# Batch-owned buffers, seven shared PSUM banks, and one searched order for all engines in a four-stage attention kernel

## The chip, the cores and the metric

The kernel runs on one core of one Trainium2 chip. The metric is device time in microseconds (us), the median of several runs; lower is better. The core has TensorE (PE, with a separate record for its weight loads), VectorE (DVE), ScalarE (ACT) and GpSimd (POOL), each with its own instruction stream in program order, and SyncE (SP), which here issues most of the DMAs.

## The reference

Four batches (B = 4) of 256 tokens with 128 channels go through attention layers with 16 heads of 8 channels. Cut to what is computed:

```python
x = attn0(x, ctx) + x                        # rotary positions on q and k, softmax over 256 keys
mod = silu(ctx[:, :2]) @ ada_w + ada_b       # 9 vectors for each half: shift, scale, gate, three times
x0, x1 = halves of x (128 tokens each)
xh = xh + g_msa * mha(mod(ln(xh)))           # each half attends to itself (128 keys)
xh = xh + g_mca * mha(mod(ln(xh)), other)    # each half attends to the other half
xh = xh + g_mlp * (gelu(mod(ln(xh)) @ fc1) @ fc2)
x = ln(attn3(x, ctx) + x) * g + b            # softmax over 256 keys
x = x + attn4(ln(x) * g + b, ctx)            # weights quantised to -1, 0, 1 times their mean size
```

So there are five attentions per batch, called phases 0 to 4 below. Phases 1 and 2 are those on halves. A pair (phase, batch) is a unit; there are 20.

## The kernel before

**One unit.** q and k are projected (fp32), and each is split into three bf16 parts. Six DMAs for q and six for k place the parts in every eighth partition of `q_stack` and `k_stack`, in pairs that make up an fp32 product (`SLOTS`), two more slots being constants that were loaded at the start (`in_spare`). A bank (128 x 512 fp32 in PSUM) of products q k is made by PE from 64 partitions, the next bank from the other 64. DVE takes its row maxima (`neg_max`, L1294). There are 16 such banks in a unit of phases 0, 3 and 4 and 8 in one of phases 1 and 2, 256 in all. The maxima are split into two bf16 parts (`max_parts`, L715 and L717), transposed by PE, copied out (L727 or L1205) and placed by DMA in two rows of `q_stack`. Then PE makes the scores with keys on partitions (`ps_score`, 256 banks), ACT takes their exponentials (`probs`, L1155, 8 buffers), and PE multiplies with `v_cols` in column tiles of 32 (`ps_heads`, `value`, 160 steps of 4 products). Then come a copy (L1162), the transpose `unstack`, the division (L1363, L1364), `heads_t`, the output projection `out_proj`, the addition of `base` (L1374), the statistics of the norm (L1258 to L1263), the reciprocal deviation on POOL (L908), the norm itself (`normed`, L735, on DVE in phases 0 to 2 and on POOL in phase 3) and its transpose `norm_t`, from which the next phase of that batch starts.

**Order.** `make_schedule` builds one list of steps by a planner with fixed costs (`Plan`) that always takes the ready step that is earliest after a bonus per stream (`WEIGHTS`). Every engine runs its part of that one list in order; much of what DVE, ACT and POOL do has no place of its own but stands where the PE step that feeds it stands. Units come in a fixed order: all batches of phase 0, then of phase 1, and so on.

**Buffers.** They go by the unit's turn: two of `neg_max`, parts, `base`, three of the stacks and of `v_cols`, one of `heads_raw`, `heads`, `normed`. The PSUM banks are private to a kind of work: three for `ps_max`, two for `ps_score`, one for `ps_heads`, two for all else (`ps_small`).

**Start and gates.** The rotary table's rows are gathered by 8 indirect DMAs (16 floats per token), widened on DVE (L1302) and transposed by PE. The three gates of each of 8 batch halves are a product with a replicated silu (`silu_rep`), 8 times [128 x 384]; POOL then multiplies them into `gated_o` and `gated_fc2` (`gate_fold`, L877 to L883).

Nearly all products of PE are recorded at L937, the helper `mm`; they are told apart by their tiles.

Of the kernel before, what the change touches and what calls it, by code (L numbers as in the profile page):

```python
# [22 lines left out]
UNITS = PHASES * B  # L23
# [3 lines left out]

UNIT = tuple((phase, b) for phase in range(PHASES) for b in range(B))
PHASE = tuple(phase for phase, b in UNIT)
BATCH = tuple(b for phase, b in UNIT)  # L30
AT = {unit: u for u, unit in enumerate(UNIT)}
BEFORE = tuple(AT.get((phase - 1, b)) for phase, b in UNIT)

SLOTS = ((0, 2), (1, 1), (2, 0), (0, 1), (1, 0), (0, 0))


ROW_SLOTS = 8
SPARE_SLOTS = (6, 7)
HALF = P // 2
MAX_ROW = HALF - 2  # L40
STACK_BUFS = 3
BANK = 512
CHUNK = BANK
SMALL_BUFS, MAX_BUFS, SCORE_BUFS = 2, 3, 2
# [24 lines left out]
ROPE_COLS = 2 * DH  # L69


def halves(u):

    return PHASE[u] in (1, 2)


def n_banks(u):
    return PAIRS if halves(u) else 2 * PAIRS


def n_chunks(u):
    return PAIRS if halves(u) else H


def n_groups(u):

    return 2 if u in GROUPED else 1


def quad_of_chunk(n):  # L90

    u = 0
    while n >= n_chunks(u):
        n -= n_chunks(u)
        u += 1
    return u, n * 4 // n_chunks(u)


def on_dve(work, u):

    return (work, PHASE[u]) in ON_DVE


def splitter(kind, u):

    return "dve" if (kind, PHASE[u]) in SPLIT_ON_DVE or u < 1 else "pool"

OFF_PE = {"norm": None, "apply": None, "stats": None, "max_split": None, "stack_max": None, "expand": None,  # L110
          "split_q": "pool", "split_k": "pool", "gate_fold": "pool", "quantise": "pool",
          "stack_q": "dma", "stack_k": "dma"}

LAG = {"pe": 200, "act": 180, "dve": 130, "pool": 70, "dma": 2150}
# [4 lines left out]
            "max_t0": 270, "max_t1": 270}  # L121


ROW_BANK, ROW_ISSUE, DRAIN = 225, 12, 170


class Plan:
# [8 lines left out]
    def run(self, engine, after, cost, gelu=False):  # L136

        if engine == "act" and gelu != self.gelu:
            self.gelu, cost = gelu, cost + 1300
# [1328 lines left out]
```

## Time and profile before

| what | us |
|---|---|
| median of 3 runs | 361.76 (361.42 to 364.45) |
| the profiled execution: its span, first to last instruction | 356.7 |
| between that span and the median | 5.1 |

The page of the profile gives busy time per engine, the span in slices, and the costliest groups of instructions. Busy time of PE counts each product with its modelled latency, so a PE that is called busy may still be waiting for most of that time. The granted clock (PEclk) is 1.00 where TensorE has 2.4 GHz and 0.50 where it has 1.2 GHz; a window's figure is the mean of the two.

### The profile page before, as it was taken

How to read it: one execution, taken by the hardware profiler on the slowest of the kernel's cores; microseconds unless marked ns; L12 is line 12 of the kernel's file. 1: busy time of each engine (PE TensorE's matmuls, PEld its weight loads, DVE VectorE, ACT ScalarE, POOL GpSimd, SP SyncE). 2: the span in 40 equal slices, each digit the busy share in tenths (PEclk: the TensorE clock that was granted, in tenths of full speed). 3: DMA queues.
4: the chain of work that ended last, by engine and by line, in shares of the span. 5: the costliest groups of instructions: out<-in, count | busy, mean ns of one | idle time of the engine just before them, and what ended most of it. 6: DMA issues, size and time to landing. Idle time of an engine off the chain costs nothing.

```text
span 356.7 us, 8841 instructions
## 1 busy us (share of the span) xinstructions
PE 303.9 (85%) x3162; PEld 169.3 (47%) x3162; DVE 246.3 (69%) x551; ACT 233.3 (65%) x491; POOL 187.3 (53%) x273
## 2 busy tenths in 40 slices
PE   3187899789899689788988989899888999898993
PEld 2173444345436466556666656455343534344331
DVE  2679599989746657758738487857686879778411
ACT  1131275767878378576768586787787777676782
POOL 3876498968888555336254332403676675740000
PEclk9587699999999899899899989879999999999999
DMA  2769700303032122133132111200212112130000
GB/s 70 184 164 244 249 9 5 83 10 79 16 83 68 33 75 75 50 77 91 27 91 54 39 47 48 60 9 19 74 38 58 51 41 69 37 78 18 17 17 16
DMA packets 40563, 22.95 MB, mean 64 GB/s; under 512 B 4872, under 2 KB 39688, under 8 KB 40392
## 3 DMA queue, kind: packets, MB, share of 16 engines
q1 hardware_dynamic: 39832, 22.30, 23.9%
q8 instruction: 25, 0.41, 0.5%
q0 software_dynamic: 256, 0.07, 0.2%
q14 instruction: 18, 0.15, 0.1%
q10 hardware_dynamic: 432, 0.02, 0.1%
HBM read 5.79 MB, written 0.52 MB: 18 GB/s over the span
## 4 chain that ended last, share of the span: by engine, by line
PE 30%; DVE 6%; ACT 6%; POOL 5%; issue 5%; SPq 1%; DMA 1%; POOLq 0%; ACTq 0%; DVEq 0%
PE ps_small L937 9%; PE ps_heads L937 7%; PE ps_max L937 5%; PE ps_score L937 5%; POOL normed L735 3%; ACT probs L1155 2%; DVE neg_max L1294 2%; PE ps_small L1108 2%; POOL rstd L908 1%; PE ps_small L1112 1%; DVE stats L1258 1%; PE ps_small L1122 1%; SPq L793 1%; DVE normed L735 1%; ACT L1228 1%
## 5 line engine op out<-in xcount | busy, mean ns | idle before, releaser
L1294 DVE TENSOR_REDUCE neg_max<-ps_max 128x2 f32<-128x512 f32 (+1 forms) x256 | 159.8, 682 | 38.4 <-PE ps_max L937 37.7
L1155 ACT ACTIVATE probs<-ps_score 128x512 f32<-128x512 f32 x256 | 141.4, 600 | 29.5 <-PE ps_score L937 28.5
L937 PE MATMUL ps_score<-q_stack,k_stack 64*128 64x256 bf16 (+1 forms) x640 | 78.8, 258 | 6.6 <-ACT probs L1155 4.3
L937 PE MATMUL ps_heads<-probs,v_cols 128*32 128x256 f32 (+1 forms) x1280 | 83.1, 350 | 0.6 <-ACT probs L1155 0.4
L937 PE MATMUL ps_max<-k_stack,q_stack 62*128 62x256 bf16 (+1 forms) x640 | 72.0, 259 | 7.9 <-DVE neg_max L1294 4.1
L937 PEld LDWEIGHTS ps_score<-q_stack,k_stack 64*128 64x128 bf16 x640 | 34.1, 96 | 40.9 <-ACT probs L1155 29.0
L937 PEld LDWEIGHTS ps_max<-k_stack,q_stack 62*128 62x128 bf16 x640 | 33.3, 96 | 41.2 <-DVE neg_max L1294 22.8
L937 PEld LDWEIGHTS ps_heads<-probs,v_cols 128*32 128x32 f32 x1280 | 28.3, 109 | 25.4 <-issue 17.3
L702 POOL TENSOR_TENSOR split_r<-q_f,k_parts 128x256 f32<-128x256 f32 x19 | 12.8, 673 | 46.2 <-issue 41.9
L937 PE MATMUL ps_small<-src_t,w 128*128 128x256 f32 x96 | 30.0, 433 | 0.9 <-issue 0.5
L908 POOL TENSOR_TENSOR rstd<-var_eps,minus_half 128x2 f32<-128x2 f32 x20 | 14.2, 708 | 30.8 <-DVE var_eps L1263 30.6
L702 POOL TENSOR_TENSOR split_r<-q_f,q_parts 128x256 f32<-128x256 f32 x19 | 12.7, 670 | 24.6 <-issue 23.2
L937 PEld LDWEIGHTS ps_small<-src_t,w 128*128 128x128 f32 x96 | 17.8, 207 | 8.7 <-issue 4.6
L1181 ACT ACTIVATE q_f<-ps_small,vec 128x256 f32<-128x256 f32 x32 | 15.2, 474 | 9.6 <-PE ps_small L937 9.2
L1219 ACT ACTIVATE src_t<-ps_small,mods 128x128 f32<-128x128 f32 x24 | 9.7, 453 | 15.2 <-PE ps_small L1122 15.2
L902 POOL TENSOR_TENSOR base<-x,rows 128x256 f32<-128x256 f32 x12 | 8.7, 726 | 19.0 <-DVE x L1374 18.2
L1363 DVE RECIPROCAL inv_sum<-ps_small 128x32 f32<-128x32 f32 x20 | 7.0, 352 | 15.6 <-PE ps_small L1108 15.3
L1162 ACT ACTIVATE heads_raw<-ps_heads 128x512 f32<-128x512 f32 x20 | 12.0, 602 | 5.5 <-PE ps_heads L937 5.1
L937 PE MATMUL ps_small<-ctx_t,w 128*128 128x256 f32 x32 | 11.5, 471 | 4.8 <-DMA ctx_t<-in_ctx_t 4.2
L1122 PE MATMUL ps_small<-ident_f,normed 128*128 128x128 f32 x32 | 6.9, 298 | 9.5 <-DVE normed L735 8.0
L1108 PE MATMUL ps_small<-ident_f,heads_raw 128*128 128x128 f32 x80 | 12.6, 280 | 2.0 <-ACT heads_raw L1162 2.0
L937 PE MATMUL ps_small<-w,ctx_t 128*128 128x128 f32 x48 | 9.2, 320 | 5.8 <-issue 5.8
(112 smaller groups left out, 420.6 us busy)
## 6 DMA issues: line engine op xcount, KB each, us to landing
k_stack<-k_parts SPq DMA_DIRECT2D x120, 64.0 KB, 2.1
q_stack<-q_parts SPq DMA_DIRECT2D x120, 64.0 KB, 2.1
w<-in_w SPq DMA_DIRECT2D x1, 1024.0 KB, 5.8
rows<-in_rows SPq DMA_DIRECT2D x1, 704.0 KB, 5.0
w<-in_w SPq DMA_DIRECT2D x1, 576.0 KB, 8.6
q_stack<-max_rows SPq DMA_DIRECT2D x36, 8.0 KB
ctx_t<-in_ctx_t SPq DMA_DIRECT2D x4, 128.0 KB, 3.5
src_t<-in_x_t SPq DMA_DIRECT2D x4, 128.0 KB, 3.6
```

The lines of the kernel that those rows point to most:

```text
L702: link(ops.tensor_tensor(rest, full, part[0], ALU.subtract))
L735: last = ops.tensor_scalar(normed[:, qt, :], src[:, qt, :], mean_var[:, qt, 0:1], rstd[:, qt:qt + 1], ALU.subtract, ALU.mult)
L902: nc.gpsimd.tensor_tensor(base[:, u % 2, :, :], x[:, b, :, :], add, ALU.add).then_inc(base_ready, 1)
L908: nc.gpsimd.tensor_tensor(rstd[:, :], var_eps[:, :], minus_half[:, :], ALU.pow).then_inc(rstd_ready, 1)
L937: return nc.tensor.matmul(out, lhs_t, rhs, start=start, stop=stop, **k)
L1108: last = nc.tensor.transpose(out[:, (qt * 2 + g) * P:(qt * 2 + g + 1) * P], heads_raw[:, g * T + qt * P:g * T + (qt + 1) * P], ident)
L1122: last = nc.tensor.transpose(out[:, qt * P:(qt + 1) * P], normed[:, qt, :], ident)
L1155: nc.scalar.activation(probs[:, n % PROB_BUFS, :], ps_score[n % SCORE_BUFS][:, :], ACT.Exp, scale=SCALE).then_inc(exped, 1)
L1162: nc.scalar.activation(heads_raw[:, :], ps_heads[:, :], ACT.Copy).then_inc(heads_copied, 1)
L1181: nc.scalar.activation(f, ps_small[:, 0:T], ACT.Identity, bias=V(f"b{kind}{phase}"))
L1219: last = nc.scalar.activation(src_t[:, b, s * P:(s + 1) * P], ps_small[:, s * P:(s + 1) * P], ACT.Identity, bias=mods[:, 2 * phase, 2 * b ...
L1294: nc.vector.tensor_reduce(dst, src, AX.X, ALU.max, negate=True).then_inc(max_taken, 1)
```

## The change

- **Order.** `Plan`, `WEIGHTS` and `make_schedule` go. `streams` names, for each batch, 40 or so sequences of steps with the engine of each, and the string `ORDER` (1919 steps of two characters, a stream and a batch) merges them. DVE's, ACT's, POOL's and SP's steps have places of their own. `BANK_OF` gives each step of PE that needs a bank one of banks 0 to 6; `value` keeps bank 7. A step waits until the reader of the step that last used its bank is done (`reader`).
- **Coupling.** Where `COUPLED` has a 1, two row steps (a bank of maxima or scores each) wait together and their products are issued alternately: 182 pairs.
- **Buffers** are indexed by batch, not by turn, so there are four of each and a batch waits for itself alone. The rotary rows share memory with `gated_o`, the table with `hidden`, `heads` with `normed`, `heads_t` with `gated`.
- **Start.** The constant slots are no longer loaded: DVE presets both stacks of each batch by two memsets of 128 x 2048 bf16, and the real parts are written over them. The first unit's q stack is placed from ACT's queue. The gathered rotary rows come wide (256 floats per token). Batches 0 and 1 and the first weights are loaded before the wait for the gathered rows; x, rows and the other weights after the first `stack_k`.
- **Gates** are one product, [8 x 384], stored to DRAM and loaded back to all partitions. fc2 keeps its own weights, and DVE multiplies its result by the gate (`add_mlp`, one more operation).
- **Engines.** The norm is on POOL in all phases, with the addition of eps; the split of the maxima is on POOL in phases 0 and 3; the rotary sum is on POOL but for the first unit. The last unit's maxima go in four groups, not two.

The core of the diff (the first two lines of `ORDER` only):

```diff
-GROUPED = (0, UNITS - 1)
-
-SPLIT_ON_DVE = ()
-ON_DVE = (("max_split", 0), ("max_split", 1), ("max_split", 2), ("max_split", 3), ("max_split", 4),
-          ("max_t", 1), ("max_t", 4),
-          ("norm", 0), ("norm", 1), ("norm", 2))
+
+
+
+FIRST, LAST = (0, 0), (PHASES - 1, B - 1)
+GROUPS = {FIRST: 2, LAST: 4}
+
+
+MAX_T_ON = ("act", "act", "act", "act", "dve")
+APPLY_ON = ("pool", "pool", "pool", "pool")
+SPLIT_MAX_ON = ("pool", "dve", "dve", "pool", "dve")
...
+ORDER = (
+    "Q0K0R0z0r0r0R1z1k0i0i0R2q000y0y00000K1z2W0r1Q1r1K2Q2d1k110r2d1w01010Q3r2q1j1M0M0M0m0m0b3M0M0m0W211i1R3i1M0112121"
+    "z3d2m0d2m0M0M0m0m0W3w3M0m0k2M0M0m0M0q2K3j1s0m0m0m0T0M0M0C0W1w1m0m0M0i2m0i230M0b2m0w2S0e0S0S0e0S0S011r3d3j221M1M1"
...
+def make_steps():
+    waiting = {letter + str(b): list(steps) for b in range(B) for letter, (_, steps) in streams(b).items()}
+    steps = []
+    for n in range(0, len(ORDER), 2):
+        kind, p, i = waiting[ORDER[n:n + 2]].pop(0)
+        steps.append((kind, p, int(ORDER[n + 1]), i))
+    assert not any(waiting.values())
+    return steps
...
+    bank_of, last_of_bank, before_in_bank = {}, {}, {}
+    table = iter(BANK_OF)
     for st in steps:
-        assert st not in order, st
-        order[st] = seen.get(st[0], 0)
-        seen[st[0]] = order[st] + 1
-
-    def no(*step):
-        return order[step]
+        if engine_of[st] != "pe" or st[0] == "value" and st[3]:
+            continue
+        bank = BANKS - 1 if st[0] == "value" else int(next(table))
+        bank_of[st], before_in_bank[st] = bank, last_of_bank.get(bank)
+        last_of_bank[bank] = st
...
+    row_steps = [st for st in steps if st[0] in ("max", "score")]
+    couple = {}
+    for n, st in enumerate(row_steps):
+        if COUPLED[n] == "1":
+            couple[row_steps[n - 1]] = st
...
+        q_stack = sb("q_stack", [P, B, PAIRS, T], BF16)
+        k_stack = sb("k_stack", [P, B, PAIRS, T], BF16)
...
+        ps = [ctx.enter_context(nc.psum_tensor(f"ps{i}", [P, BANK], F32)) for i in range(BANKS)]
...
```

and, from the engines' bodies:

```diff
+                if kind in ("stack_k", "stack_q"):
+                    place_parts(sp, kind[-1], p, b, i)
+                    if (kind, p, b, i) == ("stack_k", 0, 0, 2):
+                        load_batch(sp, 3)
...
+                        load_w(sp, 2)
+                        load_w(sp, 1)
+                        load_w(sp, 3)
...
+                if kind in ("max", "score"):
+                    row_wait(st)
+                    other = couple.get(st)
+                    if other:
+                        row_wait(other)
+                    n = 4 if halves(p) else 2
+                    for j in range(n):
+                        last = row_multiply(st, j)
...
+                        if other:
+                            last = row_multiply(other, j)
...
+            def preset_stacks(b):
+                nc.vector.memset(q_stack[:, b, :, :].rearrange("p e t -> p (e t)"), 0.0).then_inc(stacks_preset, 1)
+                nc.vector.memset(k_stack[:, b, :, :].rearrange("p e t -> p (e t)"), 1.0).then_inc(stacks_preset, 1)
+            preset_stacks(0)
...
+            nc.vector.tensor_copy(ident16[:, :], ident).then_inc(ident_ready, 1)
+            for b in range(1, B):
+                preset_stacks(b)
```

## Rows read from the trace of the kernel before

**Rows 1.** The page, part 1: busy us, share of the span, instructions.

```profile
PE 303.9 (85%) x3162; PEld 169.3 (47%) x3162; DVE 246.3 (69%) x551; ACT 233.3 (65%) x491; POOL 187.3 (53%) x273
```

**Rows 2.** Windows: us, busy (instructions) per engine, PEclk, DMA share, GB/s.

```profile
0.00:54.00 54.00, 36.20 (x195) 20.86 (x197) 37.14 (x80) 16.64 (x38) 35.71 (x53) 0.81 0.57 152
54.00:87.00 33.00, 29.45 (x296) 14.91 (x298) 30.13 (x59) 22.56 (x50) 26.73 (x36) 1.00 0.17 42
87.00:141.00 54.00, 47.01 (x609) 27.49 (x601) 34.12 (x84) 39.11 (x87) 38.77 (x64) 0.97 0.23 59
141.00:194.00 53.00, 45.58 (x626) 32.75 (x624) 35.95 (x88) 36.91 (x82) 23.98 (x36) 0.94 0.25 65
194.00:236.00 42.00, 38.41 (x366) 22.73 (x364) 29.01 (x61) 29.57 (x61) 12.80 (x19) 0.88 0.18 46
236.00:332.00 96.00, 88.87 (x902) 43.21 (x903) 75.43 (x172) 73.40 (x150) 48.57 (x68) 1.00 0.18 45
332.00:357.00 25.00, 18.43 (x186) 7.38 (x183) 4.50 (x12) 15.15 (x29) 0.72 (x1) 0.96 0.06 17
```

**Rows 3.** Waits: engine, what waited <- for what: us in total, times, longest.

```profile
PEld ps_score L937 <- ACT probs L1155: 29.0, 72, 1.6
...
PEld ps_max L937 <- DVE neg_max L1294: 22.8, 59, 1.5
```

**Rows 4.** Groups by form: count | busy, mean ns of one | idle before, releaser.

```profile
L883 POOL TENSOR_TENSOR gated_fc<-w,gates 128x512 f32<-128x512 f32 x8 | 10.1, 1268 | 0.0
...
L937 PE MATMUL ps_small<-w,silu_rep 128*128 128x384 f32 x16 | 8.6, 636 | 0.0
...
L735 DVE TENSOR_SCALAR normed<-x,mean_var,rstd 128x128 f32<-128x128 f32 x16 | 6.9, 475 | 3.8 <-POOL rstd L908 3.8
...
L735 POOL TENSOR_SCALAR normed<-x,mean_var,rstd 128x128 f32<-128x128 f32 x8 | 6.3, 794 | 0.4
...
L830 POOL MEMSET v_cols<- 128x1024 f32 x3 | 2.9, 958 | 0.1
...
L1273 DVE COPY silu_rep<-silu 128x1024 f32<-128x1024 f32 x1 | 0.7, 695 | 0.1
```

**Rows 5.** Timeline of the first 50 us: start, us, engine and line, operation.

```profile
11.66 0.60 ACT L1166 ACTIVATE rope_cs<-ps_heads 128x512 f32<-128x512 f32 x1 [7.20 <-PE ps_heads L1046]
...
15.99 1.89 SPq L793 DMA_DIRECT2D k_stack<-k_parts  x3
...
23.69 0.59 SPq L796 DMA_DIRECT2D rows<-in_rows  x1
...
27.61 4.86 DVE L1294 TENSOR_REDUCE neg_max<-ps_max 128x2 f32<-128x512 f32 x8
...
34.30 2.73 PE L937 MATMUL ps_small<-silu,w 128*128 128x8 f32 x12
...
44.24 10.15 DVE L1294 TENSOR_REDUCE neg_max<-ps_max 128x2 f32<-128x512 f32 x16
...
47.34 1.08 ACT L1155 ACTIVATE probs<-ps_score 128x512 f32<-128x512 f32 x2
```

**Rows 6.** Timeline of PE alone, about 246 us.

```profile
246.01 0.40 PE L937 MATMUL ps_score<-q_stack,k_stack 64*128 64x256 bf16 x4
246.24 0.60 PE L937 MATMUL ps_max<-k_stack,q_stack 62*128 62x256 bf16 x6
246.77 0.64 PE L937 MATMUL ps_heads<-probs,v_cols 128*32 128x256 f32 x8
247.41 0.39 PE L937 MATMUL ps_max<-k_stack,q_stack 62*128 62x256 bf16 x2
```

**Rows 7.** Timeline of the end.

```profile
331.16 1.88 DVE L1294 TENSOR_REDUCE neg_max<-ps_max 128x2 f32<-128x512 f32 x3
...
347.60 1.09 ACT L1155 ACTIVATE probs<-ps_score 128x512 f32<-128x512 f32 x2 [0.29 <-PE ps_score L937]
...
354.03 0.42 DVE L1374 TENSOR_TENSOR x<-ps_small,base 128x256 f32<-128x256 f32 x1 [1.93 <-PE ps_small L937]
```

More of the change, by code:

```diff
@@ L22 @@
 PHASES = 5
-UNITS = PHASES * B
 MAX_POS = 512
 PARTS = 3
[L28 to L34, printed above, removed]
+SLOTS = ((0, 2), (0, 1), (0, 0), (1, 0), (2, 0), (1, 1))
 ROW_SLOTS = 8
-SPARE_SLOTS = (6, 7)
 HALF = P // 2
 MAX_ROW = HALF - 2
-STACK_BUFS = 3
@@ L55, with engines @@
+def make_steps():
[6 more added lines that the diff above has]
+    return steps
+def engines():
+    return {(kind, p, b, i): engine for b in range(B) for engine, steps in streams(b).values() for kind, p, i in steps}
 W_NAMES = ["k0", "k0r", "q0", "q0r", "v0", "o0",
@@ L676, in half_rows, with parts_of @@
+        def parts_of(kind, b):
+            return [(q_parts if kind == "q" else k_parts)[:, b, j, :] for j in range(PARTS)]
         def half_rows(par, n=HALF):
             return slice(HALF * par, HALF * par + n)
[L680 to L687 removed]
@@ new lines, in hidden, with flat, kv_source, query_ready @@
+        def hidden(b, f):
+            at = b % 2 * 2 + f // 2
+            return rope_hidden[:, at, f % 2 * T:(f % 2 + 1) * T]
+        def flat(tile, b):
+            return tile[:, b, :, :].rearrange("p n c -> p (n c)")
+        def kv_source(p):
+            return src_t if halves(p) else ctx_t
+        def query_ready(p, b):
+            return done("take_x_t", 2, b, 0) if p == 3 else done("take_norm_t", p - 1, b, 0)
+        def part_ready(kind, p, b, part):
+            if part == 0:
+                return done("take_" + kind, p, b, 0)
+            return done("split_" + kind, p, b, part - 1)
@@ new lines, in split_part @@
+        def split_part(engine, ops, link, rest, kind, p, b, i):
+            part, full = parts_of(kind, b), q_f[:, b, 0 if kind == "q" else 1, :]
+            step = ("split_" + kind, p, b, i)
+            if i == 0:
+                engine.wait_ge(*part_ready(kind, p, b, 0))
+                ops.tensor_tensor(part[1], full, part[0], ALU.subtract).then_inc(of(step), 1)
+            else:
+                link(ops.tensor_tensor(rest, full, part[0], ALU.subtract))
+                engine.wait_ge(*part_ready(kind, p, b, 1))
+                ops.tensor_tensor(part[2], rest, part[1], ALU.subtract).then_inc(of(step), 1)
+                engine.wait_ge(*done(*step))
@@ new lines, in transpose, with row_wait @@
+            def transpose(out, src, by):
+                return nc.tensor.transpose(out, src, by)
+            def row_wait(st):
+                kind, p, b, i = st
+                if kind == "max" and i == 0:
+                    pe.wait_ge(q_placed[b], 16 * len(SLOTS) * (p + 1))
+                    pe.wait_ge(k_placed[b], 16 * len(SLOTS) * (p + 1))
+                if kind == "score" and i * n_groups((p, b)) % n_banks(p) == 0:
+                    pe.wait_ge(*placed_max(p, b, i * n_groups((p, b)) // n_banks(p)))
+                if before_in_bank[st]:
+                    pe.wait_ge(*done(*reader(before_in_bank[st])))
@@ L1035, in _ @@
+                    last.then_inc(of(st), 1)
+                    continue
+                out = ps[bank_of[st]]
+                if before_in_bank[st]:
+                    pe.wait_ge(*done(*reader(before_in_bank[st])))
+                if kind in ("k", "q"):
+                    if p == 0:
                         pe.wait_ge(qk_loaded, 16)
-                        for kind in ("k", "q"):
-                            pe.wait_ge((src_loaded if kind == "q" else ctx_loaded)[0], 16)
-                            project_roped(kind, 0, ps_smalls[no("small", kind, 0)]).then_inc(small_ready, 1)
```

1715 lines of the change are left out of this document (683 added, 1032 removed).

## Prediction, made before the changed kernel was run

> **What bounds the kernel now.** I read the totals first [rows 1]. PE is called busy for 85% of the span, DVE for 69%, ACT for 65%. That is not a PE at its limit: a product of 256 columns is recorded with its latency. I counted columns at 107 ns for 256 (two passes for fp32): 512 row banks, two at a time, stream for 55 us, the value steps for 27, everything else for about 65, so about 150 us at 2.4 GHz. So something makes PE wait, and the reader should look for what.
>
> The windows say how much [rows 2]. I cut the span where each 32 or 64 banks of maxima are done. The start (to 54 us) and the end (from 332) are special. Between them lie 278 us. In each of the five middle windows one engine other than PE has most work: DVE 30.1, ACT 39.1, ACT 36.9, ACT 29.6, DVE 75.4, in sum 211.1 us. So 67 us of the middle are waiting of the kind that a better order or more free buffers could remove, and no more than that.
>
> The waits tell where some of it is [rows 3]. PE's weight loads stop 59 times for 22.8 us until DVE has read a `ps_max` bank and 72 times for 29.0 us until ACT has read a `ps_score` bank, 0.39 and 0.40 us each. While PE stands there, work of other kinds waits behind it in program order.
>
> The rows of PE alone show a second loss [rows 6]. Two streams in the two row halves run together: the ten row products from 246.01 are two coupled banks and one single one, 3 x 0.214 = 0.64 us at 107 ns for 256 columns, and the next mode starts at 246.77, so 0.12 us go in the change of tiling. The eight value products last 0.43 us and `ps_max` follows after 0.64. In other places of the trace it is 0.57 against 0.43. I take 0.12 us per change of mode. The mean granted clock of the middle is 0.96, so 1.2 GHz holds for some 20 us of it [rows 2].
>
> **The start.** First maxima are read at 27.61, the second unit's only at 44.24, first exponentials at 47.34 [rows 5]. DVE works 37 of 54 us, ACT 17 [rows 2]. The new kernel's first steps, worked out by the rows:
> - DVE first runs eight memsets of 128 x 2048 bf16, two before the table rows' addresses and six before the first rotary product. No such row exists. The nearest with the same bytes is the DVE copy of 128 x 1024 fp32 at 0.70 us, the only MEMSET is POOL's, 0.958 us for 1024 elements [rows 4]: 0.70 to 1.92 us each. I take 1.92, since it is the same operation, so 15.3 us. The addresses are late by 2 x 1.92 minus the wait for positions, about 0.8 us, and DVE is free at about 18 us. The table was there at 12.3 [rows 5], so the memsets and no longer the table set the start.
> - From 18: the k rotation 1.3 us, ACT's copy 0.4, q likewise to 21.3, three q DMAs from ACT's queue at 0.63 us (1.89 for three [rows 5]), splits on DVE meanwhile, three more DMAs to 25.0, landing 2.1 us: first maxima near 27 us, where they are now. By 0.70 us per memset DVE is free at 11, the table sets again, and they come at 22.
> - SP has placed k at 23.6 and then issues x, rows and 2.1 MB of weights ahead of the second unit's stacks, in one go; before they were issued from 23.69 on in two portions [rows 5]. 3.3 MB at the 150 to 250 GB/s of this stretch are through at about 38 to 41. The second unit's maxima follow at about 42 instead of 44.24. The product `mod` no longer stands in PE's way at 34.30 while its weights load, and 7 of the 8 gate products (16 records of 0.64 us, 8.6 us in all [rows 4]) are gone; these are what frees the stretch to 47.
> - Start: 3 us earlier. Bounds: 8 earlier with the cheap memset, 2 later if the second unit's stacks land last.
>
> The Trainium skill (VectorE: DVE Perf Modes, "Zero memsets can be issued as uint32 (trn2)") says that a memset takes one cycle per element whatever the dtype; with the 0.96 GHz of "Trainium Kernel Development and Optimization", NeuronCore Architecture, that is an estimate of 2.13 us each and 17.1 us for eight. By it the start would gain about 1.5 us instead of 3, by the copy's row 8.
>
> **The middle.** I counted the changes of mode (rows, columns, full array) in both lists of PE steps: 413 before and 287 after. Between the 32nd and the last bank of maxima it is 359 and 252. 107 fewer at 0.12 us are 12.8 us (0 if they all fall into waits). The coupling itself is priced at nothing: neighbouring banks already run together in [rows 6]; it costs at most that the first of two banks waits for the second's bank to be free.
>
> Seven banks that anyone may use, and buffers per batch, attack the 51.8 us of [rows 3]. PE may run ahead with maxima while exponentials lag, and the reverse, as the eight probability buffers allow. That all of it goes is impossible, for ACT's and DVE's own work stays; that none goes would need an order that uses the banks as before. I take a third, 17 us (bounds 0 and 40).
>
> Against it: the norm of phases 0 to 2 moves from DVE (475 ns) to POOL (794 ns [rows 4]), two operations in each of 12 units, on the chain from one phase of a batch to its next. That is 24 x 0.32 = 7.7 us of longer chains, the other three batches covering part of it: I take 4 us (0 to 7.7). In total POOL gains 24 x 0.794 = 19 us of norms and loses 10.1 us of fc2 folding [rows 4] and about as much of other folding, so it stays near 200 us; DVE loses 24 x 0.475 = 11 us of norms and gains 15 us of memsets, that lie ahead of its first maxima. The gates' trip through DRAM is hidden: the product stands at the 70th bank of maxima and its first use after the 80th, some 8 banks or 5 us of DVE later at least. Middle: -12.8 - 17 + 4 = -26 us.
>
> **The end.** The last bank of maxima is read by 333.0, the last exponential ends at 348.7, the last sum at 354.5, the store then lands at the span's end [rows 7]. So 15.7 us for exponentials (ACT works 15.2 of 25 us [rows 2]) and 8.0 for the chain behind. In the new order 13 exponentials follow the last maxima, 24 before, and four groups let the scores start after each quarter. 13 at 0.55 us (two take 1.09 [rows 7]) are 7.2 us; the last group's own path (split, transpose, copy, two DMA issues, landing, four exponentials) is about as long. End: -8.5 us (-3 to -10).
>
> **Sum.** 356.7 - 3 - 26 - 8.5 = 319.2 us of span; with the 5.1 us that lie between span and median, 324.3. I write 325.
>
> **Rivals.**
> - *Only what can be counted pays.* The bank waits stay, because ACT and DVE are late rather than the banks few: a bank that is free a little earlier only moves the wait to the next bank. For it: in the windows where PE waits least the busiest engine still has but 79% (75.4 of 96 us [rows 2]). Against it: 131 separate waits, with other work ready behind them. Then 356.7 - 3 - 12.8 + 4 - 8.5 + 5.1 = 341.5 us.
> - *Slower: the shared banks tie engines together.* PE takes a bank from the table 695 times, and each take waits for the last user's reader, whichever engine that is. A projection that was served by two private banks may now stand behind a late maximum. Today 131 of 512 row banks wait, 0.40 us each [rows 3]. The gain of 37 us is used up at 37 / 0.40 = 92 more waits. With 110 more, a fifth of the other 564 takes, it is 324 + 44 = 368 us. Against it: seven banks hold what seven did, and an early free bank is found for each step where the table is good.
> - *It does not do what it says.* The order is new but its idle time is the same, because the chain of each batch through POOL, DMA and norms sets the pace (three engines idle at once). Then the start's 3 and a part of the end's gain, if not eaten again, are all: 350 to 362 us, 358 as the middle of them.
> - *The start is worse.* Memsets of 1.92 us and loads ahead of the second unit's stacks cost 5 us instead of gaining 3: 332 us, inside the range.
>
> **How the numbers follow.** Forecast 0.70 (own range 303 to 340, from the bounds: 15 us less of bank waits, 5 us of a better start on the low side), only the countable 0.14, slower 0.09, the order that changes nothing 0.07. The range of 303 to 350 leaves out the slower case, most of that last case and what would lie below 303, in sum about 0.18. A change of 1% (3.6 us) is about what a measurement of this kernel can tell from none. Faster by over 1%: 0.70 + 0.14 = 0.84. Of the no-difference case I give 0.06 to within 1% and 0.01 to slower, so slower has 0.10.
>
> **What would show it.** In the new profile: first `neg_max` at 27 (at 22 if memsets are cheap) and MEMSET rows of DVE of 0.7 or 1.9 us; first `probs` near 41; the second unit's maxima near 42; PE's waits for DVE and ACT on banks near 35 us in sum, not 52; the 32nd bank at 51 and the last near 304; 15 us from the last maxima to the end. The forecast is wrong if PE's waits for banks are as long as now or sit on other kinds of work, if POOL's records touch each other over 50 us and more, or if the second unit's maxima start after 46.

## The result, and the profile after

The changed kernel takes 330.0 us (median of 4 runs, 328.07 to 332.44), the kernel before 361.6 us (median of 4 runs, 356.23 to 364.45). The ratio is 0.920, with a 95% interval of 0.912 to 0.929; this ratio and those below are taken from fast executions alone, so they need not be the quotient of the two medians. The profiled execution has a span of 326.2 us, where before had 356.7.

The page's totals of the kernel after, in the form of [rows 1]:

```profile
PE 271.0 (83%) x3152; PEld 160.8 (49%) x3152; DVE 231.1 (71%) x494; ACT 223.0 (68%) x485; POOL 200.9 (62%) x331
```

DVE has 15 us less work, ACT 10 us less, POOL 14 us more. None of the three was near the length of the span, before or after. PE is recorded as busy for 33 us less, but its products did not become shorter: the 1280 row products last 258 ns in the mean before and 257 after, the 1280 value products 350 and 349, and only the time that they cover fell, from 150.8 to 118.6 us for maxima and scores (each counted by itself) and from 83.1 to 73.6 for values. They lie closer together. Of the rest, 8.6 us were the gate products. So most of the 30 us did not come from less work on a full engine. To see where they went, I split both traces by the start of the 1st, 33rd, 65th, ... read of a maximum (`neg_max`, counted in the timeline of DVE):

| start of the read of a maximum, us | 1st | 33rd | 65th | 97th | 129th | 161st | 193rd | 225th | 256th | end |
|---|---|---|---|---|---|---|---|---|---|---|
| before | 27.6 | 55.2 | 91.0 | 147.2 | 200.3 | 238.4 | 274.5 | 306.6 | 332.4 | 356.7 |
| after | 28.2 | 53.5 | 85.2 | 141.1 | 191.8 | 221.9 | 252.8 | 285.0 | 309.7 | 326.2 |

The stretch to the 33rd read is 1.7 us shorter, the middle (33rd to last) 256.2 instead of 277.2 us, so 21.0 less, and the end 16.5 instead of 24.3, so 7.8 less. Windows cut at these points, after (columns as in [rows 2]):

```profile
0.00:53.50 53.50, 34.67 (x236) 19.64 (x238) 41.26 (x75) 17.61 (x41) 30.14 (x51) 0.84 0.53 158
53.50:85.20 31.70, 28.79 (x272) 14.87 (x266) 24.57 (x53) 19.21 (x40) 13.73 (x25) 0.78 0.20 52
85.20:141.10 55.90, 44.27 (x650) 28.78 (x645) 31.22 (x77) 40.19 (x93) 40.36 (x68) 1.00 0.34 88
141.10:191.80 50.70, 42.66 (x638) 30.28 (x638) 30.35 (x70) 40.23 (x91) 41.58 (x67) 1.00 0.28 70
191.80:221.90 30.10, 28.62 (x304) 19.00 (x300) 25.37 (x51) 24.62 (x51) 21.79 (x38) 1.00 0.19 49
221.90:309.70 87.80, 79.25 (x932) 40.69 (x932) 72.50 (x158) 70.95 (x153) 53.35 (x87) 1.00 0.18 47
309.70:326.20 16.50, 12.78 (x147) 7.53 (x136) 5.83 (x17) 10.18 (x21) 0.00 (x0) 1.00 0.11 33
```

Two things are to be seen here. The long window from 221.9 has DVE busy for 83% of its time (72.50 of 87.80), before it was 79% in the last window of [rows 2]'s middle. And the granted clock is 1.00 from 85 us on, where [rows 2] had 0.97, 0.94 and 0.88. In sum, before has 20.5 us at half clock in its middle and after 13.7, all of that between 57 and 71 us. So the middle has 6.8 us less at half clock, which is worth at most half of that, 3.4 us.

PE's waits for the two big readers, after (columns as in [rows 3]; L675 makes the maxima, L676 the scores):

```profile
PEld ps L675 <- DMA q_stack<-q_parts: 14.0, 13, 2.4
...
PEld ps L676 <- ACT probs L848: 10.4, 24, 0.9
...
PEld ps L675 <- ACT probs L848: 7.3, 18, 0.8
...
PEld ps L676 <- DVE neg_max L970: 5.9, 17, 0.8
...
PEld ps L675 <- DVE neg_max L970: 4.9, 13, 0.6
```

The four bank rows are 28.5 us in 72 waits, against 51.8 us in 131 of [rows 3], and no wait is longer than 0.9 us, where 1.6 was. Maxima now wait for exponentials and scores for maxima, which private banks could not do. Products of other kinds (transposes, projections) wait another 8.9 us for these two readers, where the kernel before had none, so in sum it is 37 us against 52. (The value products, which keep a bank of their own, wait 5.0 us for exponentials, 4.4 before.) What has grown is the first row: maxima wait for the DMA that brings the q parts, 14.0 us against 5.1.

### The profile page after: what moved, and what is told of

Same layout as the page of the kernel before. It is cut to its first block, busy times and chain, and to the rows that moved or that the text cites. A ratio compares the mean times of both kernels' runs of the same rounds, so it can differ in the third digit from the quotient of the medians.

```text
span 326.2 us, 8882 instructions
## 1 busy us (share of the span) xinstructions
PE 271.0 (83%) x3152; PEld 160.8 (49%) x3152; DVE 231.1 (71%) x494; ACT 223.0 (68%) x485; POOL 200.9 (62%) x331
## 4 chain that ended last, share of the span: by engine, by line
PE 49%; DVE 10%; issue 9%; ACT 9%; SPq 8%; DMA 8%; POOL 7%; POOLq 0%; ACTq 0%
PE ps L718 11%; PE ps L675 8%; PE ps L676 8%; SPq L463 7%; DVE neg_max L970 7%; PE ps L646 6%; ACT probs L848 5%; DMA q_stack<-q_parts 5%; PE ps L744 4%; PE ps L806 2%; PE ps L711 2%; PE ps L754 2%; PE ps L816 2%; PE ps L823 2%; POOL k_parts L474 1%
## 5 line engine op out<-in xcount | busy, mean ns | idle before, releaser
L970 DVE TENSOR_REDUCE neg_max<-ps 128x2 f32<-128x512 f32 (+1 forms) x256 | 160.0, 683 | 41.7 <-PE ps L675 41.1
L848 ACT ACTIVATE probs<-ps 128x512 f32<-128x512 f32 x256 | 133.5, 610 | 23.0 <-PE ps L676 21.4
L675 PE MATMUL ps<-k_stack,q_stack 62*128 62x256 bf16 (+1 forms) x640 | 59.6, 259 | 13.5 <-DMA q_stack<-q_parts 8.9
L676 PE MATMUL ps<-q_stack,k_stack 64*128 64x256 bf16 (+1 forms) x640 | 59.0, 255 | 9.5 <-DMA q_stack<-max_rows_split 2.3
L718 PE MATMUL ps<-probs,v_cols 128*32 128x256 f32 x768 | 55.6, 397 | 0.9 <-ACT probs L848 0.8
L675 PEld LDWEIGHTS ps<-k_stack,q_stack 62*128 62x128 bf16 x640 | 28.6, 96 | 41.0 <-DMA q_stack<-q_parts 14.0
L676 PEld LDWEIGHTS ps<-q_stack,k_stack 64*128 64x128 bf16 x640 | 28.4, 95 | 34.9 <-ACT probs L848 10.4
L718 PEld LDWEIGHTS ps<-probs,v_cols 128*32 128x32 f32 x768 | 19.9, 111 | 19.6 <-issue 9.5
L868 ACT ACTIVATE q_f<-ps,vec 128x256 f32<-128x256 f32 x32 | 15.2, 474 | 17.2 <-PE ps L744 16.9
L559 POOL TENSOR_SCALAR var_eps<-mean_var 128x2 f32<-128x2 f32 x20 | 4.6, 229 | 27.5 <-DVE mean_var L1019 27.1
L492 POOL TENSOR_SCALAR heads_normed<-x,mean_var,rstd 128x128 f32<-128x128 f32 x24 | 19.2, 807 | 1.3
L646 PE MATMUL ps<-ident_f,heads_normed 128*128 128x128 f32 x72 | 14.7, 291 | 5.5 <-DVE heads_normed L1000 3.5
L744 PE MATMUL ps<-src_t,w 128*128 128x256 f32 x48 | 17.1, 444 | 1.9 <-ACT src_t L899 1.1
L711 PE MATMUL ps<-probs,v_cols 128*32 128x128 f32 x512 | 18.0, 276 | 0.2 <-ACT probs L848 0.2
L711 PEld LDWEIGHTS ps<-probs,v_cols 128*32 128x32 f32 x512 | 12.8, 109 | 3.5 <-ACT probs L848 1.5
```

The source lines that it names most:

```text
L492: last = ops.tensor_scalar(heads_normed[:, b, qt, :], src[:, b, qt, :], mean_var[:, b, qt, 0:1], rstd[:, b, qt:qt + 1], ALU.subtract, ALU. ...
L646: return nc.tensor.transpose(out, src, by)
L675: return nc.tensor.matmul(out, queries, keys, start=True, stop=True)
L676: return nc.tensor.matmul(out, keys, queries, start=True, stop=True)
L711: last = nc.tensor.matmul(ps[BANKS - 1][32 * j:32 * j + 32, g * T + at * P:g * T + (at + 1) * P], v_cols[:, b, keys_tile(p, at), h, :], pr ...
L718: last = nc.tensor.matmul(ps[BANKS - 1][32 * j:32 * j + 32, g * T:(g + 1) * T], v_cols[:, b, at, h, :], pr[:, at * T:(at + 1) * T], start= ...
```

## The experiments

Each run shows its median and its ratio to the kernel before on the same chip. The kernel before itself had medians of 356 to 362 us from chip to chip, so small differences are taken between kernels of one chip: the first four kernels below ran on one, the next four on another, then three on the first again, and the last on a third.

**1. The old order on everything new.** The planner's list of before, step by step, on the new buffers, start, gates and engines; banks private.

```diff
-GROUPS = {FIRST: 2, LAST: 4}
+GROUPS = {FIRST: 2, LAST: 2}
-ORDER = ("Q0K0R0z0r0r0R1z1k0i0i0R2q000y0y0...
+ORDER = ("K0Q0R0z0r0k010r0q000i0i01010W0w0...
 # BANK_OF: 0-2 for maxima, 3-4 for scores, 5-6 for the rest; COUPLED: all 0
```

> The changed kernel's buffers, start, gates and division of work among the engines, but the order of steps that the planner of the kernel before made (translated step by step; last unit's maxima in two groups, nothing coupled), and private banks: three for maxima, two for scores, two for the rest. Theory A (the order of the steps, together with banks that suit it, brings nearly all of the gain): 361.6 - 2 for the start + 4 for the norms on POOL - 0 = about 362 us, range 355 to 370, with about 413 changes of mode. Rival B (buffers owned by batches, the new start and the single gate product bring it, the order is mere decoration): 335 to 345 us.

Measured: 374.0 us, ratio 1.049 (1.037 to 1.062). It is slower than the kernel before, and 44 us slower than the changed kernel. Its windows from 93 us on:

```profile
93.40:154.40 61.00, 50.12 (x648) 30.56 (x644) 30.73 (x71) 39.92 (x91) 44.10 (x74) 0.92 0.21 55
154.40:210.00 55.60, 48.66 (x612) 33.92 (x610) 29.81 (x70) 39.27 (x86) 30.66 (x48) 0.92 0.24 60
210.00:248.20 38.20, 33.68 (x318) 19.83 (x316) 25.28 (x51) 26.72 (x55) 15.26 (x26) 0.91 0.17 43
248.20:345.90 97.70, 88.27 (x892) 41.59 (x894) 73.40 (x158) 71.84 (x146) 51.36 (x81) 0.98 0.17 44
345.90:370.20 24.30, 18.10 (x182) 7.27 (x180) 4.17 (x12) 14.81 (x29) 0.00 (x0) 0.96 0.06 17
```

DVE's and ACT's work in the first four of these windows is that of the changed kernel within 2.1 us (73.40 and 71.84 against 72.50 and 70.95 in the longest), but every window is longer, by 5.1, 4.9, 8.1, 9.9 and 7.8 us. PE's waits are those of before:

```profile
PEld ps L676 <- ACT probs L848: 28.8, 69, 1.5
PEld ps L675 <- DVE neg_max L970: 23.2, 46, 2.1
```

So buffers, start, gates and engines bring nothing by themselves; rival B falls. The order of steps, with banks that suit it, is worth 44 us on this base: 31 in the middle, 8 at the end and 5 ahead of the 33rd read of a maximum, since the first maxima come only at 32.4 us here. It is not the clock: an execution of this kernel with a mean granted clock of 0.924 took 372.1 us, one of the changed kernel with 0.922 took 332.4.

**2. The old order with seven shared banks.**

```diff
 # as 1, but
-BANK_OF: by kind
+BANK_OF: of the seven, the bank whose reader stands earliest in the list
```

> The same old order, but with the seven shared banks, each step taking the bank whose reader comes earliest in the list. Theory A: sharing alone brings little, since the old order starts each kind of work only about as far ahead as its private banks allow: within 5 us of the run with private banks. Rival C (the shared banks themselves take away the waits): 15 to 20 us less than with private banks, since PE's 52 us of waits for row banks would fall by a third. Rival D (sharing ties the engines together): more than 5 us slower than with private banks.

Measured: 372.8 us, ratio 1.044 (1.035 to 1.052), so the same as 1 within the intervals. In time, C and D both fall. But the waits did not stay as they were:

```profile
PEld ps L675 <- DVE neg_max L970: 8.8, 19, 1.8
...
PEld ps L646 <- ACT probs L848: 7.5, 9, 1.7
PEld ps L646 <- DVE neg_max L970: 7.3, 6, 2.9
...
PEld ps L676 <- ACT probs L848: 4.5, 14, 0.4
```

Row products wait 22.9 us for the two readers, where run 1 had 52.0. Products of other kinds (L646 are transposes) wait 24.1 us for them, where run 1 had none, and value products 10.6 instead of 4.4. In sum it is 58 us against 56: sharing alone moved the waits to other work and brought no time. So the mechanism of D is there, engines tied together by shared banks, but not its price. Nor is the time spent at the same places: the first maxima come at 27.7 instead of 32.4 us, the stretch to the 33rd read is 3.1 us shorter and the middle 8.9 longer. How much of the latter the banks make stays open, for this trace is of an execution of 377.0 us.

I had meant to run the new order on private banks as well. Its list keeps up to six maxima and six scores at once between product and reader, and needs all seven banks together at 11 places. Played through on the list with three, two and two banks used in turn, it stops for good in the first unit: PE waits for a bank whose reader stands, in DVE's list, behind a maximum that PE has yet to make. So this order does not go with that division, and its gain was not divided between order and sharing.

**3. No coupling.**

```diff
-COUPLED = ("0101000000100000010100100000010010...
+COUPLED = ("0000000000000000000000000000000000...
```

> The changed kernel with no pair of row steps coupled: every bank's products are issued by themselves, in the same order of steps. My prediction priced coupling at nothing: 330 +- 2 us, since neighbouring banks in different row halves run together anyway. Rival: only alternating issue lets the two row halves run together; then 182 pairs lose up to 0.2 us each, about 36 us, of which the part on PE's path would be seen: 340 to 366 us.

Measured: 327.8 us, ratio 0.916 (0.906 to 0.927), span 326.2 as with coupling. Coupling is worth nothing that can be measured. The rival of 340 to 366 us falls: the two row halves run together also when one bank's products are issued behind another's.

**4. Four changes at the start.**

```diff
+            load_batch(sp, 3)                          # SP: before the first k parts
-            for b in range(1, B):                      # POOL: not ahead of everything
-                clear_v(b)
+                    if st == ("split_k", 0, 0, 1):     # but behind the first split
+                        for n in range(1, B):
+                            clear_v(n)
-                nc.vector.memset(k_stack[...], 1.0)
+                nc.vector.memset(k_stack[...].bitcast(F32), BF16_ONES)   # two ones in a word
-            for b in range(1, B):                      # DVE: each batch's presets
-                preset_stacks(b)
+                        preset_stacks(...)             # behind the first units' rotary sums
```

> The changed kernel with four changes in its start: batch 3's x is loaded with batch 2's, before the first k parts are placed (PE stands behind q of batch 3 otherwise); POOL clears the value columns of batches 1 to 3 only after the first unit's parts are split; DVE presets the stacks of batches 1 to 3 one by one behind the first unit's work; the ones are set as fp32 words (128 x 1024 elements). Theory A (the first maxima at 28.2 us are late by these presets, clears and loads, and what follows is shifted with them): first maxima at 22 to 24 us, median 325 to 327, so 3 to 5 us less than the changed kernel. Rival E (what the start wins is lost before the 32nd bank of maxima, since the second unit's loads or PE's work set that point): first maxima earlier, but 329 to 331 us.

Measured: 328.3 us, ratio 0.918 (0.909 to 0.928). Against run 3 on the same chip nothing is gained, and the first maxima were read at 27.5, not at 22 to 24. The timeline says why:

```profile
24.90 0.81 PE L677 MATMUL ps<-k_stack,q_stack 62*128 62x256 bf16 x10 [1.45 <-DVE heads_normed L990]
...
25.60 0.91 DVE L937 MEMSET q_stack<- 128x1024 uint32 x1 [0.16 <-issue]
...
26.67 0.91 DVE L938 MEMSET k_stack<- 128x1024 f32 x1 [0.16 <-issue]
...
27.50 1.82 DVE L970 TENSOR_REDUCE neg_max<-ps 128x2 f32<-128x512 f32 x3
```

PE was ready at 24.9, but DVE stood in front of its reads with the presets that I had moved there. That is a fault of my edit; run 12 mends it.

**5 and 6. The price of a change of mode.** 48 one-column products inside runs of row products, on the full array (each makes two changes), and as control in the row tiling.

```diff
+                    if st in extra:
+                        nc.tensor.matmul(ps[bank_of[st]][:, 0:1], ident16[:, :], ident16[:, 0:1], start=True, stop=True)
 # control: k_stack[half_rows(i % 2), b, 0, 0:P], q_stack[half_rows(i % 2), b, 0, 0:1]
```

> The changed kernel with 48 products of one column on the full array put inside runs of row products (into a bank whose first columns the next step writes anew), so 96 more changes of tiling; nothing is left out. Theory A (each change of mode costs PE about 0.12 us, and PE is on the path most of the time): 96 x 0.12 = 11.5 us and 48 x 0.06 = 3 us of the products themselves, 12 to 15 us if all of it is on the path; I expect 6 to 14 us over the changed kernel. Rival F (changes of mode fall into waits and cost nothing, so the 12.8 us of my sum were not there): within 3 us of the control with row products.

> Control of the other: the same 48 products of one column, at the same places, but in the row tiling of their neighbours, so no more changes of mode. Both theories: 48 x 0.03 to 0.06 us = 1.5 to 3 us at most, so 330 to 333 us. The difference to the run with full-array products is the price of 96 changes of mode.

Measured: 333.3 us, ratio 0.937 (0.932 to 0.942), and the control 330.2 us, ratio 0.928 (0.925 to 0.932). The 96 changes cost 3.1 us, with some 2 us of uncertainty either way, so 0.03 us each (0.01 to 0.06) and not 0.12. The records of the added products, full array and then control (in the groups of costliest instructions; idle time before them behind the bar):

```profile
L695 PEld LDWEIGHTS ps<-ident 128*128 128x128 bf16 x48 | 4.6, 96 | 11.0 <-issue 6.5 <-ACT probs L855 2.1 <-DVE neg_max L977 1.3
```

```profile
L695 PEld LDWEIGHTS ps<-q_stack,k_stack 64*128 64x128 bf16 x48 | 4.5, 95 | 4.8 <-ACT probs L855 1.5 <-issue 1.4 <-DVE neg_max L977 0.6
```

The idle time of the kind "issue" ahead of them is 6.5 us against 1.4: 5.1 us for the 48 changes into the full array, 0.11 us each, which is the 0.12 of [rows 6] again. So the price exists where PE goes from one mode to the next, but only a part of it reaches the end. That idle time which was there anyway takes up the rest is the likely reason; it was not tested by itself.

**7. The norms of phases 0 to 2 on DVE again.**

```diff
+        if kind == "apply" and i == 1 and p < 3:
+            out.append(("rstd", p, b, 1))              # POOL: reciprocal deviation alone
+            continue
+        if kind == "norm_t" and p < 3:
+            out.append(("apply", p, b, 1))             # DVE: the norm, ahead of its transpose
```

> The changed kernel with the norm's two halves of phases 0 to 2 back on DVE (24 operations); POOL makes only the reciprocal deviation there. Theory A (my sum): the longer norms on POOL cost 4 us, so this one is 2 to 6 us faster, 324 to 328. Rival G (the other batches cover the norm, and DVE, nearest to full, pays for 24 x 0.475 = 11 us of work and for waits that stand in its way): 0 to 8 us slower, 330 to 338.

Measured: 345.0 us, ratio 0.971 (0.966 to 0.975): 15 us slower than the changed kernel, nearly twice the worst that I had allowed. The norm of it that took longest from its statistic, on DVE and POOL:

```profile
211.93 0.25 DVE L1040 BATCH_NORM_AGGREGATE mean_var<-stats 128x2 f32<-128x6 f32 x2
...
212.57 0.72 POOL L576 TENSOR_TENSOR rstd<-var_eps,minus_half 128x2 f32<-128x2 f32 x1
...
214.89 4.47 DVE L991 TENSOR_REDUCE neg_max<-ps 128x2 f32<-128x512 f32 x7
...
219.27 1.05 DVE L508 TENSOR_SCALAR heads_normed<-x,mean_var,rstd 128x128 f32<-128x128 f32 x2
...
220.47 0.41 PE L667 MATMUL ps<-ident_f,heads_normed 128*128 128x128 f32 x2 [1.52 <-DVE heads_normed L508]
```

And one of the changed kernel, on POOL:

```profile
195.86 0.72 POOL L560 TENSOR_TENSOR rstd<-var_eps,minus_half 128x2 f32<-128x2 f32 x1
196.69 1.82 POOL L492 TENSOR_SCALAR heads_normed<-x,mean_var,rstd 128x128 f32<-128x128 f32 x2
```

The deviation is there at 213.3, but an addition and seven maxima stand before the norm. From the last statistic to the norm's end the 12 units of phases 0 to 2 took 4.5 us in the mean (1.8 to 8.1) here, 3.1 (2.8 to 4.0) in the changed kernel, and 3.1 (1.7 to 5.1) in the kernel before. POOL's slower norm is no later; it is never over 4.0 us, so it hardly queues.

**8. The last unit's maxima in two groups, not four.**

```diff
-GROUPS = {FIRST: 2, LAST: 4}
+GROUPS = {FIRST: 2, LAST: 2}     # two turns of max_split, max_t, stack_max left out of ORDER
```

> The changed kernel with the last unit's maxima in two groups of eight banks instead of four of four; the rest of the order is the same. Theory A: the scores of the last unit start later, and ACT's exponentials behind the last maxima grow from 13 towards 16 with the transposes' and the DMAs' path of 5 us before them: 2 to 6 us slower, 332 to 336. Rival H: the end is set by the new order alone and the groups bring nothing: 329 to 331.

Measured: 331.9 us, ratio 0.932 (0.926 to 0.937); the control of run 6, on the same chip but with 48 more products, had 0.928 (0.925 to 0.932). The end after the start of the last maximum's read is 17.5 us instead of 16.5. So the traces give the four groups about 1 us. In time this is not resolved: 331.9 lies between the ranges of the two theories, and the intervals overlap. Most of the shorter end is there with two groups as well, so it comes with the order.

**9. Norms on DVE, but placed two DVE steps behind their statistics.**

```diff
-        if kind == "norm_t" and p < 3:
-            out.append(("apply", p, b, 1))
+        if on.get(st) == "dve":    # two further DVE steps passed since ("stats", p, b, 0)
+            out.append(("apply", p, b, 1))
```

> As the run with the norms of phases 0 to 2 on DVE, but each norm stands two steps of DVE behind its statistics, not right before the transpose that needs it. In the other run (345.0 us) the time from the last statistic to the end of the norm was 4.5 us in the mean (1.8 to 8.1), against 3.1 us on POOL (2.8 to 4.0) in the changed kernel: DVE's norm stood behind its maxima. Theory J (that queueing is what made it slower, and the engine's speed hardly matters): mean near 3 us, and 328 to 334 us in all. Theory A (my sum: 0.32 us less for each of 24 norms gives 4 us): 324 to 327. Rival K (any work of DVE between the maxima delays PE's next banks, wherever it stands): 338 or more.

Measured: 337.4 us, ratio 0.949 (0.940 to 0.959). The time from statistic to norm fell to 2.8 us in the mean (1.8 to 4.8), so better than on POOL, and yet the kernel stays 7 us slower than the changed one. J explains half of run 7's loss (345.0 to 337.4). The other half fits K: an operation of DVE between its maxima delays banks, which the same operation on POOL does not. Row products wait 32.8 us for the two readers here, 28.5 in the changed kernel. The time lies between the ranges of J and K. The clock does not explain these two runs, though this run has 34 us of its middle at half clock, run 7 has 44 and the changed kernel 13.7: executions of this run with mean clocks of 0.939 and 0.929 took 336.9 and 337.4 us, those of run 3 on the same chip with 0.936 and 0.932 took 324.2 and 328.0; run 7 took 346.6 at 0.916, run 6 on its chip 330.5 at 0.922.

**10. The same for the old order.** Norms on DVE in run 1, at the place where the kernel before had them.

```diff
 # as 1, and
+        if kind == "apply" and i == 1 and p < 3:
+            out.append(("rstd", p, b, 1))
+        out.append(st)                                 # "apply" is DVE's now
```

> The old order with private banks on the new buffers (374.0 us), but with the norms of phases 0 to 2 on DVE again, at the place in the order where the kernel before had them. Theory A (the norms on POOL cost this order 4 to 8 us of the 13 us by which it is slower than the kernel before): 366 to 370 us. Rival L (the rest of the new division of work or the start is what costs the old order its time): 372 to 376 us.

Measured: 369.6 us, ratio 1.033 (1.024 to 1.043), so 4.4 us less than run 1 by the medians, though the two intervals overlap a little. The mean time from the last statistic to the norm's end is 2.7 us here and 3.5 in run 1. In the old order the norms on POOL do cost about what my sum said; in the new order they save 7 us or more against both places on DVE that I tried. The sign depends on the order. What makes the rest of the 12 us by which this run is slower than before is open; 5 us of it stand ahead of the first maxima (32.7 against 27.6), and these go with the private banks, for run 2, with the same start, read its first at 27.7.

**11. Another table of banks for the new order.**

```diff
-BANK_OF = ("0122201340241356041345615346156...
+BANK_OF = ("0123456210345216045241652146521...   # the bank whose reader stands earliest
```

> The changed kernel with its order of steps, but another table of banks: each step takes, of the seven banks, the one whose reader stands earliest in the list. Theory M (with this order any sensible choice of bank will do, the table was not where the gain is): 328 to 332 us. Rival N (the table was found together with the order and the times of the readers; a bank whose reader is first in the list is not the first to be free, since the readers are on three engines): 335 to 345 us, with PE's waits for banks over 50 us.

Measured: 338.3 us, ratio 0.946 (0.938 to 0.955), about 8 us slower than the changed kernel. Waits of PE, to be held against the four bank rows of the changed kernel:

```profile
PEld ps L676 <- DVE neg_max L970: 10.7, 21, 1.1
PEld ps L676 <- ACT probs L848: 8.3, 21, 0.9
PEld ps L675 <- DVE neg_max L970: 7.7, 20, 0.7
PEld ps L675 <- ACT probs L848: 6.9, 19, 0.8
```

33.6 us instead of 28.5, and 14.8 instead of 8.9 for the other kinds: in sum 48 against 37 us. Rival N holds in its time: the table matters, and this plainer one costs 8 us. Its reason, that the reader which stands first in the list is not first in time when the readers are on several engines, fits the longer waits but was not tested by itself. (That the waits would be over 50 us was a little too much.)

**12. The start mended, without coupling.** The x of batch 3 early, POOL's clears late, ones as words, all presets ahead of DVE's first sum, as in the changed kernel.

```diff
 # the edits of 4 without the last (preset_stacks stays where it was), and COUPLED of 3
```

> The uncoupled kernel (327.8 us) with three changes in the start: batch 3's x loaded before the first k parts are placed, POOL's clearing of the other value columns behind the first unit's splits, and the ones of the k stacks preset as fp32 words, all eight presets still ahead of DVE's first rotary sum (in the run with four changes at the start two pairs of presets stood ahead of the first maxima, which were read at 27.5 though PE had made them at 24.9). Theory A (an earlier first unit shifts all that follows): first maxima at 22 to 24 us, the 32nd bank at 50 to 51, 323 to 326 us. Rival E (the start of the second unit and PE's clock set the 32nd bank): first maxima at 22 to 24 us, but the 32nd bank again at 53 to 55 and 327 to 329 us.

Measured: 322.7 us (6 runs), ratio 0.903 (0.897 to 0.908). That beats both kernels. From the timeline:

```profile
23.57 0.39 PE L677 MATMUL ps<-k_stack,q_stack 62*128 62x256 bf16 x2
24.00 0.69 DVE L972 TENSOR_REDUCE neg_max<-ps 128x2 f32<-128x512 f32 x1 [0.31 <-PE ps L677]
```

The first maxima are read 3.6 us earlier than in run 3 (24.0 against 27.6), the 33rd 2.1 us (52.3 against 54.4), and the median is 5 us less. A stretch at half clock from 34 to 48 us takes back a part of the earlier start; such a stretch is there without the edits too (33 to 50 us in run 3, 40 to 47 in the changed kernel). So Theory A holds in size, though the 3 us that came behind the 33rd read cannot be told from the variation of chips and clock: behind it this trace has 10.2 us at half clock and run 3 has 17.1.

## Why the prediction was right, and where it was not

The total was right, 325 for 330, with all three stretches gaining as forecast: -3, -26 and -8.5 us, measured -1.7, -21.0 and -7.8, so the span is 326.2 us where I had 319.2. What stood behind the middle's number was only partly right. Its largest counted term was some 9 us too high, another had the wrong sign for this order, and that the errors went opposite ways is luck.

- **Changes of mode, -12.8 us: mis-sized by a factor of about four.** The count was fine, and so was 0.12 us as the time that PE idles. The step that failed is that all 107 were laid on the path. Runs 5 and 6 give 0.03 us each, so 3.5 us (1 to 6), if changes that are taken away from the old order count like those that were added to the new one.
- **Bank waits, -17 us: the waits as expected, their price not shown.** I expected PE's waits for banks near 35 us in sum; they are 28.5 for rows and 8.9 for other kinds. Runs 1, 2 and 11 show what brings the time: the order (44 us on the same buffers, whether the old order has private or shared banks) and a table of banks that fits it (8 us). I took a third of the waits as a gain of "order and banks" without saying that the banks without the order bring nothing: run 2 took 29 us off the waits of row products, more than I had hoped for, and gained no time. What the 15 us of waits that went are worth by themselves, no run shows. With 3.5 us for the modes and at most 3.4 for the clock, some 14 of the middle's 21 us are left for the order and what came with it.
- **Norms on POOL, +4 us: wrong sign in this order.** I charged 24 x 0.32 us of longer operations and left out the queue that a norm has on DVE. In the old order the sum holds (run 10: 4.4 us); in the new one the norms on DVE cost 7 (run 9) and 15 us (run 7). Against the kernel before, the way from statistic to norm is neither longer nor shorter, 3.1 us in both.
- **Coupling at nothing: right** (run 3).
- **The clock: left out.** I read 20 us at half clock in the middle and gave no term for it. After 85 us it is gone, but 13.7 us stand ahead of that, so 6.8 us went and 3.4 us is the most that the clock can have brought to the middle. As a whole the gain is not the clock's: the kernel before took 356.25 us in an execution with a mean clock of 0.953 (on the chip of run 12), the changed kernel 328.07 with the same.
- **The start, -3 us: 1.7 came, and not by my working.** The eight memsets:

```profile
L936 DVE MEMSET k_stack<- 128x2048 bf16 x4 | 7.1, 1765 | 1.5 <-issue 1.5
...
L935 DVE MEMSET q_stack<- 128x1024 uint32 x4 | 3.6, 912 | 1.5 <-PEq L1121 1.0 <-issue 0.5
```

They sum to 10.7 us, not 15.3, with 2 us of idle time between them, and DVE was free at 15.2, not 18. The four over zeros ran at half the length of those over ones, where I had taken one price for all. What this won was lost again at a place where I had not looked: the first maxima stand on PE behind the q projection of batch 3, whose x is loaded behind the first k parts on SP.

```profile
26.06 0.75 PE L733 MATMUL ps<-src_t,w 128*128 128x256 f32 x2 [3.52 <-DMA src_t<-in_x_t]
...
28.24 5.47 DVE L970 TENSOR_REDUCE neg_max<-ps 128x2 f32<-128x512 f32 x9 [4.00 <-PE ps L675]
...
41.81 1.29 DVE L970 TENSOR_REDUCE neg_max<-ps 128x2 f32<-128x512 f32 x2 [0.83 <-PE ps L675]
```

  First maxima 28.2 (I had 27), the second unit's 41.8 (42), first exponentials 40.0 (41), the 33rd read 53.5 (I had 51 for the 32nd). Run 12 shows what that one queue position, POOL's clears and the cheaper ones were worth: about 5 us.
- **The end, -8.5 us: right,** 16.5 us where I had 15.2. I gave the four groups a share in it; the trace of run 8 leaves them 1 us. The rest goes with fewer exponentials that remain: 14 start behind the start of the last read of a maximum, 24 before, and they end 7.7 us after it instead of 15.7 (columns as in [rows 7]):

```profile
309.08 1.29 DVE L970 TENSOR_REDUCE neg_max<-ps 128x2 f32<-128x512 f32 x2 [0.26 <-PE ps L675]
...
314.06 4.03 ACT L848 ACTIVATE probs<-ps 128x512 f32<-128x512 f32 x8 [0.20 <-PE ps L676]
...
323.54 0.42 DVE L1007 TENSOR_TENSOR x<-ps,base 128x256 f32<-128x256 f32 x1 [1.23 <-PE ps L806]
```

- **The work of the engines.** By my sum DVE was to gain 4 us, and it lost 15; for POOL the 187.3 + 19 and less 20 make 186, not the near 200 that I wrote and that came (200.9). I had left out that the split of the maxima and the rotary sum move from DVE to POOL.
- **From span to median, +5.1 us.** This is no fixed distance. In every execution whose span is on record beside its time, the time is 1.8 to 1.9 us more; the rest is how far the profiled execution lay from the median, and for the changed kernel the whole is 3.8.
- **The rivals.** "Only what can be counted pays" would have kept the 52 us of bank waits; they fell to 37. "Shared banks tie engines together" is real as a mechanism: waits across kinds appeared (7.3 and 5.9 us), with a plainer table the kernel is 8 us slower, and in run 2 they ate all that shorter waits of row products could bring, but never came the 37 us that this rival needed. "The order changes nothing" is turned round by runs 1 and 2: without the new order nothing is gained, and what came with it costs the old order 12 to 17 us.

## What to carry to other kernels

When several engines each run half or three quarters full and none is the bound, the order in which their streams are merged can be worth more (here 44 of 374 us) than new buffers, banks and a new division of work without it; test those with the old order before crediting them. A wait that gets shorter is no gain until it is seen where the time went: shared banks took 29 us of waiting off one kind of work and put it on others. Idle time seen at a mode change, or a longer operation on a slower engine, is a cost only as far as no other waiting covers it: ask what the operation queues behind on either engine, and price it on the path, not by its record. Before a start is tuned, look at what stands ahead of the first product on PE and ahead of its data on the load queue, one by one.

## What the runs showed of the hardware that I had not expected

- A memset on DVE was recorded by elements, not bytes. Zeros over 128 x 2048 bf16 ran as 128 x 1024 uint32 in 0.912 us, ones over the same shape in 1.765 us as bf16, and in 0.91 us when written as fp32 words that hold two ones (run 4).
- The records put 0.11 us of idle time ahead of a weight load that enters the full array from row tiling, beyond what a load in the same tiling has (runs 5 and 6), while the kernel becomes only 0.03 us longer for each change.
- The slower kernels mostly spend more of their middle at half clock: 13.7 us in the changed kernel (330 us), 34 in run 9 (337), 44 in run 7 (345). Which of the two is the cause was not tried, and it is no rule: runs 4 and 5 have 27 us at 328 and 333 us. Executions of one and the same kernel differ too: the changed kernel had mean clocks from 0.953 (328.1 us) to 0.922 (332.4 us).
